# VectorE instead of GpSimd adds the input to the weighted heads in a gated-attention and quantized-FFN kernel

## What is computed

```python
hn = (h - mean) * rsqrt(var + 1e-6) * outnorm_weight      # per head, h from the attention over ctx
x  = x + hn.reshape(B, S, E)                              # the first residual
m, v = x.mean(-1), x.var(-1)
y  = (x - m) / sqrt(v + 1e-5)                             # layer norm
q  = clip(round(y * s), -128, 127) / s,  s = 127 / max|y| # per token
h  = silu(q @ Wg.T) * (q @ Wu.T)                          # Wg, Wu, Wd rounded to -1, 0, 1 times a scale
x  = x + quant(h) @ Wd.T                                  # the second residual
```

## Time and profile before

| | before |
|---|---|
| three executions, us | 659.87, 662.36, 663.27 |
| the profiled execution, us | 657.75 |
| its span, us (first to last instruction) | 655.9 |
| busy: PE | 567.0 us, 86% |
| busy: DVE | 541.9 us, 83% |
| busy: ACT | 476.4 us, 73% |
| busy: POOL | 295.2 us, 45% |
| granted TensorE clock, mean | 0.999 of full |

### The profile page before, as it was taken

How to read it: one execution, slowest core, us unless ns; L and a number is a source line. 1 busy time by engine, 2 the same in 40 slices (tenths; PEclk the granted TensorE clock), 3 DMA queues, 4 the chain that set the end, 5 groups by cost and what they waited for, 6 DMA issues and landing times. The chain is left out here.

```text
span 655.9 us, 12646 instructions
## 1 busy us (share of the span) xinstructions
PE 567.0 (86%) x3566; PEld 365.2 (56%) x3566; DVE 541.9 (83%) x1442; ACT 476.4 (73%) x716; POOL 295.2 (45%) x475
## 2 busy tenths in 40 slices
PE   1825557799999999999999999999999998899995
PEld 0824444376566665576647656666557664455442
DVE  3149777998989898989899898989898889988763
ACT  1878776587858796788768785879678876855653
POOL 2012436544664546463564466454646346334200
PEclk9999999999999999999999999999999999999999
DMA  8944724101234102620252123410171041000001
GB/s 330 376 137 159 273 91 147 47 2 49 82 94 165 49 18 74 218 77 0 81 176 80 48 81 116 140 48 30 64 219 55 0 161 48 33 17 12 22 17 48
DMA packets 34208, 63.74 MB, mean 97 GB/s; under 512 B 2688, under 2 KB 19200, under 8 KB 31616
## 3 DMA queue, kind: packets, MB, share of 16 engines
q1 hardware_dynamic: 33600, 62.92, 28.0%
q10 hardware_dynamic: 576, 0.44, 0.3%
HBM read 54.84 MB, written 8.52 MB: 97 GB/s over the span
## 5 line engine op out<-in xcount | busy, mean ns | idle before, releaser
L573 PE MATMUL GU<-WQ,xqT 128*128 128x512 bf16 x1024 | 239.4, 381 | 6.6 <-DVE FF L1184 6.5
L573 PEld LDWEIGHTS GU<-WQ,xqT 128*128 128x128 bf16 x1024 | 97.2, 98 | 109.0 <-issue 6.5
L603 PE MATMUL ACC<-WQ,FF 128*128 128x512 bf16 x512 | 115.8, 379 | 2.9 <-ACT FF L829 2.9
L810 ACT ACTIVATE FF<-GU,cgu 128x512 f32<-128x512 f32 x128 | 86.7, 690 | 21.0 <-PE GU L573 19.3
L1184 DVE TENSOR_TENSOR FF<-FF,GU 128x512 f32<-128x512 f32 x128 | 85.1, 680 | 15.3 <-ACT FF L810 12.3
L603 PEld LDWEIGHTS ACC<-WQ,FF 128*128 128x128 bf16 x512 | 49.4, 98 | 59.3 <-ACT FF L829 3.7
L818 ACT ACTIVATE FF<-FF,magic,hs 128x1024 f32<-128x1024 f32 x64 | 79.2, 1242 | 3.1 <-DVE hs L1215 3.1
L776 ACT ACTIVATE work<-AT,pb 128x128 f32<-128x128 f32 x128 | 48.1, 455 | 15.8 <-POOL pb L1480 15.3
L520 PE MATMUL AT<-vext,CT 128*128 128x129 f32 x256 | 51.7, 295 | 4.7 <-ACT gate_parts L714 3.8
L1500 POOL TENSOR_TENSOR work<-work,norm_bc 128x512 f32<-128x512 f32 x32 | 41.8, 1306 | 23.8 <-ACT work L776 23.8
L1466 POOL TENSOR_SCALAR pb<-den 128x4 f32<-128x4 f32 x32 | 7.0, 218 | 98.7 <-DVE den L1122 98.7
(11 more groups left out here) (117 smaller groups left out, 1201.4 us busy)
## 6 DMA issues: line engine op xcount, KB each, us to landing
bc<-gate_rows SPq DMA_DIRECT2D x32, 512.0 KB, 6.4
xin<-in_x SPq DMA_DIRECT2D x32, 256.0 KB, 2.8
kT<-in_ctx_t SPq DMA_DIRECT2D x8, 1024.0 KB, 4.8
vext<-in_ctx SPq DMA_DIRECT2D x32, 256.0 KB, 3.5
out<-FF SPq DMA_DIRECT2D x32, 256.0 KB, 2.3
WQ<-in_w_gate SPq DMA_DIRECT2D x4, 1024.0 KB, 13.0
FF<-in_w_up SPq DMA_DIRECT2D x4, 1024.0 KB, 15.5
FF<-in_w_down SPq DMA_DIRECT2D x4, 1024.0 KB, 4.7
```

Of the source, the lines that this page charges most:

```text
L573: last = nc.tensor.matmul(dst, xqT[:, b, P * k:P * (k + 1)], w[:, k, 512 * j:512 * (j + 1)], start=(k == 0), stop=(k == KC - 1))
L603: last = nc.tensor.matmul(ACC[:, :], hT[:, b % 2, P * k:P * (k + 1)], WD[:, k, :], start=(k == 0), stop=(k == JT - 1))
L810: nc.scalar.activation(sg[:, j % 2, :], GU[:, 2 * (j % 2), :], ACT.Silu, scale=cgu[:, b, 0:1]).then_inc(silu_done, 1)
```

## The change

The sum moves from POOL to DVE. `residual` on POOL becomes `weigh_heads`, which keeps the product with the norm weight and posts `x1_ready` after it. DVE's `x1_stats` waits for `x1_ready` as before, does the sum itself, waits for its end, and goes on with the statistics. POOL's calls stand where they stood.

```diff
@@ x1_stats, VectorE @@
                 dve.wait_ge(x1_ready, g * 4 + (b + 1))
+                V.tensor_tensor(xin[:, bass.ds(slot, 1), b, :], work[:, b % 2:b % 2 + 1, :], xin[:, bass.ds(slot, 1), b, :],
+                                ALU.add).then_inc(dve_seq, 1)
+                s = count.next()
+                dve.wait_ge(dve_seq, s)
                 V.bn_stats(st_2[:, :], xin[:, bass.ds(slot, 1), b, :]).then_inc(dve_seq, 1)
@@ GpSimd @@
-            def residual(g, b, slot):
+            def weigh_heads(g, b):
 
                 if absent(g):
                     return
                 pool.wait_ge(at_out, at_use(f"num{b}", g))
-                G.tensor_tensor(work[:, b % 2, :], work[:, b % 2, :], norm_bc[:, :], ALU.mult).then_inc(pool_seq, 1)
-                s = count.next()
-                pool.wait_ge(pool_seq, s)
-                G.tensor_tensor(xin[:, bass.ds(slot, 1), b, :], work[:, b % 2:b % 2 + 1, :], xin[:, bass.ds(slot, 1), b, :],
-                                ALU.add).then_inc(x1_ready, 1)
+                G.tensor_tensor(work[:, b % 2, :], work[:, b % 2, :], norm_bc[:, :], ALU.mult).then_inc(x1_ready, 1)
@@ iteration, GpSimd (the same for the other three tiles) @@
-                residual(former, 1, slot_former)
+                weigh_heads(former, 1)
```

More of the change, by code:

```diff
@@ L1518, in iteration @@
                 former, now, coming = it - 1, it, it + 1
-                slot_former = slot_of(former)
-                slot_now = slot_of(now)
                 x_rstd(coming, 0)
@@ L1528, in iteration @@
                 fade_state(former, 2)
-                residual(former, 2, slot_former)
+                weigh_heads(former, 2)
                 weigh_keys(now, 0)
@@ L1534, in iteration @@
                 x_rstd(coming, 1)
-                residual(former, 3, slot_former)
+                weigh_heads(former, 3)
                 x1_rstd(former, 3)
@@ L1546, in iteration @@
                 weigh_q(now, 3)
-                residual(now, 0, slot_now)
+                weigh_heads(now, 0)
                 x1_rstd(now, 0)
```

## The result

The changed kernel is slower by 3.2%: a median of 681.82 us over four executions (679.39 to 686.22) against 661.12 us for the kernel before in the same comparison, ratio 1.0322 (95% interval 1.0288 to 1.0356). The forecast was 675 us and slower by 1.9%; direction and range hold, the size was 12.7 us where 20.7 us were measured. The profiled execution took 683.49 us (span 681.4 us).

A forecast was written before the change was run, and what follows sets the result against it. DVE was taken to bound it as tightly as PE. Per steady group 2.88 - 0.76 - 0.3 = 1.8 us; six give 11, plus 0.7 (group 0) and 1 (group 7): 12.7 us on 662.36, so 675 us; range 662 to 687 us.

The forecast's parts named there:

- What bounds the kernel: Steady stretch: DVE taken for about 69.4 of 71 us, as tightly as PE; relieving POOL is worth nothing by itself.
- The price of a sum, 0.72 us: Each sum added on DVE ahead of the statistics delays all behind it by 0.72 us, 2.88 us per group.
- Rival 3: Added DVE sums held behind POOL operations, 0.83 us more each; half of 32 hit gives 688 us; chance 0.10.
- The gaps: DVE's waits at L1117 (0.5 us), L1060 (0.2) and ahead of tile 3 (0.06) take in 0.76 us per group.
- The one of 0.9 us at `multiply`: DVE's wait at L1184 begins at DVE's own instruction 10 us earlier, so it stays and takes in nothing.
- The relief at the port, -0.3 us: At L1048, a later DVE loses less behind POOL's product: 0.3 us per group given back, between 0 and 0.7.
- the shift of `weigh_keys`: POOL's operation behind tile 1 starts at about 311.3 instead of 312.81 us; nobody waits for it in the steady stretch.
- PE can't stand in the way, and its waits grow by as much: PE, with 2.85 us of idle in a group, does not limit; its waits grow by the group's 1.8 us.
- Filling and drain: Of 2.88 us each, group 0 costs 0.7 us and group 7 costs 1 us, as DVE's waits there absorb part.
- No change: DVE's idle time takes in the sums: 666 us, or 662 us if small waits absorb too; chance 0.16.
- faster: A tile's way from `norm_heads` to the statistics gets 0.95 us shorter, in filling and drain: 655 us; chance 0.08.
- Rival 4: No absorption, ACT and PE being late by as much: each of 32 sums costs 0.72 us, 685 us; chance 0.16.

The follow-up runs named there:

- e2: Kernel before with POOL's sum and the wait ahead of it left out, no sum on DVE: 663.91 us, ratio 1.0017.
- f3: Kernel before without any first-residual sum, POOL's product of tile 1 held until DVE's gate rows are done: 656.41 us, ratio 0.9944.
- e8: Kernel before with POOL's product of tile 1 held until DVE's gate rows are done: 659.72 us, ratio 0.9983.
- e7: Changed kernel with POOL's product of tile 1 held until DVE's gate rows are done: 674.70 us, ratio to before 1.0214.
- f1: Changed kernel with 14 spare PE transposes ahead of the wait for tile 3's rounded input: 679.25 us, ratio to before 1.0285.
- e5: Kernel before, POOL's sum kept, with a second sum of the same form on DVE into `work`: 700.73 us, ratio 1.0611.
- e3: Kernel before with the sum moved to DVE for tile 3 of each group alone: 667.04 us, ratio 1.0075.

## Why the prediction was right, and too small

**What bounds the kernel.** Right. DVE was taken for nearly the whole period, and 6.4 us of idle time by the windows took in 0.9 us of 2.88. The removal alone (e2) brought nothing in its time; only with the order at the port held did it bring something, 0.5 us a group (f3).

**The price of a sum, 0.72 us.** Right: 0.72, 0.72, 0.73 us in the offsets, 684 ns each, and none of the 32 was held at the port. Rival 3 put the lock on the added sums; it struck elsewhere.

**The gaps.** 0.76 us were counted as taken in; measured 0.11 + 0.55 + 0.14 us at tile 3 + 0.08, 0.88 us. The one of 0.9 us at `multiply` stayed, as argued. With the hold in both kernels, e8 to e7, it is 1.8 us a group where 2.88 - 0.76 is 2.1; the difference is what POOL's sum and `cgu` cost e8 ahead of tile 3's statistics.

**The relief at the port, -0.3 us.** This step failed, in its sign. L1048 was held for 0.9 us, and I reckoned that a later DVE loses less there. It looked at one instruction: a DVE that is 0.6 us later meets the product with the instruction in front of it, L1044, which had just slipped through before, and L1048 then meets `weigh_keys`, which comes earlier, because POOL's sum and its pause no longer stand in between. It was +0.6 us. The prediction had the shift of `weigh_keys` from 312.81 to about 311.3 us in front of it and wrote that nobody waits for it; nobody did, but it holds a port. With that the group would have been 2.7 us longer, as measured.

**The clock.** It isn't in the sum. "PE can't stand in the way, and its waits grow by as much" took PE's idle time for free. Its gaps of over 0.25 us add up to 2.0 to 2.5 us in a group before and to 4.8 to 5.0 us after, and in three of five groups of the profiled execution the clock fell, 1.8 us each. So a term of 5.4 us there was put at nothing. That the waits are its cause agrees with f1 and is not proven.

**Filling and drain.** Group 0 was put at 0.7 us; in the profile it cost 3.75 us, about 2.4 us by the sums (the waits for ACT's weights took in only the first of them) and the rest behind a clock that was down from 134 to 138 us. The clock was down in group 0 of e2's trace too, where DVE has no sum at all, so those 1.4 us need not come from the change. Group 7 was put at 1 us and cost 0.2 us.

Put together for the profiled pair: 1.2 us are there before the first sum is reached (a longer wait for the first constants, not the change), 3.75 us in group 0, 20.4 us in the six steady groups of which 5.4 us come with the fallen clock, and 0.2 us in the drain, 25.5 us in all. The medians differ by 20.7 us; the profiled execution of the changed kernel lies 1.7 us above its median and that of before (657.75 us) 3.4 us below 661.12 us, which makes up the rest.

**The range.** The measured 682 us is at the upper edge of what the prediction gave to its own mechanism (669 to 682 us), and it is reached with the sign at the port turned round and with the clock added, so that the number came out inside owes something to the width of the range.

**The rivals.** No change and faster are out. Rival 4, that nothing is absorbed, gives the nearest figure (685 us), but for a reason that isn't so: about 0.8 us a group were absorbed, and the port and the clock took it back.

## What to carry to other kernels

Where two engines share a port, an operation that moves or goes changes who comes first at every later meeting, so cost the instructions around it as pairs in time, in both directions, and not only the one that is held now. An engine that "isn't waited for" can still hold another: delaying POOL's product by a wait of no urgency gave 7 us in the changed kernel and 2 us in the one before. And don't take more idle time of TensorE for free: look at the granted clock behind its waits, which here cost 1.8 us in a group where it fell.

## What the runs showed of the hardware

- The same 16x128 scan (L1044) and sum (L1048) on DVE take 0.47 and 0.28 us alone, and 1.31 and 1.34 us where a POOL product or sum had started ahead of them; a `tensor_scalar` from SBUF to SBUF (L996) goes from 0.53 to 1.32 us in the same way. The Trainium skill, SBUF — State Buffer, "Who interferes with whom", says that the one which issues first has the port for its whole instruction; the trace agrees, a lead of 0.17 us was enough (e2).
- Statistics (L1149), products with one input in PSUM (L1188) and reductions (L1163, L1196) never showed it: the longest took 0.70, 0.69, 0.69 and 1.22 us, each within 0.02 us of its median, in the changed kernel and in e5. One reduction L1163 ran from 278.84 us on, under a product of POOL that had begun at 278.56 us.
- PE at 1.2 GHz took 3.33 us for eight matmuls that take 1.9 us at 2.4 GHz. Waits of 1.17 and 0.69 us at the end of an iteration were followed by a lower clock in three groups of the changed kernel and not in the last steady one (1.18 and 0.69 us), nor in any of e3; what decides this stays open.
